# Gated experts: gathered rows split first, then turned by transposing DMA transfers instead of TensorE

## The reference, cut to what matters

```python
affinity = _sinkhorn(affinity_logits)
gates, idx = jax.lax.top_k(affinity, CAP)
expert_in = jnp.take_along_axis(x[:, None, :, :], idx[..., None], axis=2)
h = jax.nn.gelu(jnp.einsum('becd,edf->becf', expert_in, w1) + b1[None, :, None, :])
expert_out = jnp.einsum('becf,efd->becd', h, w2) + b2[None, :, None, :]
out = out.at[jnp.arange(b)[:, None, None], idx].add(gates[..., None] * expert_out)
```

## Time and profile before

| | us |
|---|---|
| median of 3 runs | 2324.47 |
| the profiled execution | 2321.31 |
| its span, first to last instruction | 2319.5 |
| TensorE busy in the span | 2096.1 (90%) |
| VectorE busy | 1494.0 (64%) |
| ScalarE busy | 1275.3 (55%) |
| GpSimd busy | 1095.1 (47%) |

### The profile page before, as it was taken

How to read it: one execution, slowest core, us unless ns; L and a number is a source line. 1 busy time by engine, 2 the same in 40 slices (tenths; PEclk the granted TensorE clock), 3 DMA queues, 4 the chain that set the end, 5 groups by cost and what they waited for, 6 DMA issues and landing times. The chain is left out here.

```text
span 2319.5 us, 47393 instructions
## 1 busy us (share of the span) xinstructions
PE 2096.1 (90%) x17558; PEld 1475.3 (64%) x17590; DVE 1494.0 (64%) x2938; ACT 1275.3 (55%) x2080; POOL 1095.1 (47%) x1263
## 2 busy tenths in 40 slices
PE   7799999996895599978999979965999999999998
PEld 5566666663664388855666658852676676676675
DVE  5677777775996755547888846666555555555553
ACT  2576666663443366535666645534645655655653
POOL 2888888841220222126666313403555355355343
PEclk9899999997998799999999989986999999999999
DMA  5000000000002233311111000042345345344332
GB/s 234 1 2 1 0 0 0 0 1 6 10 7 73 96 121 120 116 48 35 30 28 27 0 12 17 16 146 96 94 112 112 75 111 111 77 111 108 80 81 32
DMA packets 66925, 136.11 MB, mean 59 GB/s; under 512 B 11200, under 2 KB 52368, under 8 KB 59920
## 3 DMA queue, kind: packets, MB, share of 16 engines
q1 hardware_dynamic: 37264, 87.65, 11.2%
q0 software_dynamic: 29568, 47.21, 10.1%
HBM read 100.22 MB, written 34.60 MB: 58 GB/s over the span
## 5 line engine op out<-in xcount | busy, mean ns | idle before, releaser
L3448 ACT ACTIVATE f_h<-bank,f_b 128x512 f32<-128x512 f32 x256 | 176.0, 688 | 274.6 <-PE bank L176 268.0
L3545 DVE TENSOR_TENSOR f_hidlo<-f_h,f_hidhi 128x512 f16<-128x512 f32 x256 | 177.3, 692 | 174.0 <-ACT f_hidhi L3449 174.0
L176 PE MATMUL ring<-f_w2lo,f_hidhi 128*128 128x256 f16 x1024 | 279.1, 273 | 0.0
L176 PE MATMUL ring<-f_w2hi,f_hidhi 128*128 128x256 f16 x1024 | 279.1, 273 | 0.0
L176 PE MATMUL ring<-f_w2hi,f_hidlo 128*128 128x256 f16 x1024 | 279.1, 273 | 0.0
L3648 POOL DMA_INDIRECT out<-f_y,f_to_row x128 | 205.9, 1609 | 92.6 <-DVE f_y L3563 50.8
L176 PE MATMUL bank<-f_xthi,f_w1hi 128*128 128x512 f16 x512 | 194.7, 380 | 1.1 <-DVE f_xtlo L3524 1.1
L176 PE MATMUL bank<-f_xtlo,f_w1hi 128*128 128x512 f16 x512 | 194.8, 380 | 0.0
L176 PE MATMUL bank<-f_xthi,f_w1lo 128*128 128x512 f16 x512 | 194.7, 380 | 0.0
L3449 ACT ACTIVATE f_hidhi<-bank,f_b 128x512 f16<-128x512 f32 x256 | 174.2, 680 | 0.0
L3612 POOL DMA_INDIRECT f_xg<-tokens,f_from_row x128 | 143.8, 1123 | 48.4 <-issue 34.3
(11 more groups left out here) (639 smaller groups left out, 5971.6 us busy)
## 6 DMA issues: line engine op xcount, KB each, us to landing
f_raw<-in_e_w SPq DMA_DIRECT2D x32, 1024.0 KB, 5.7
c_raw<-in_e_w SPq DMA_DIRECT2D x16, 1024.0 KB, 7.1
slots_out<-c_y SPq DMA_DIRECT2D x40, 128.0 KB, 4.2
x<-in_x SPq DMA_DIRECT2D x1, 4096.0 KB
tokens<-c_xn SPq DMA_DIRECT2D x16, 256.0 KB, 2.6
tokens<-f_xn SPq DMA_DIRECT2D x16, 256.0 KB, 2.7
out<-x SPq DMA_DIRECT2D x1, 4096.0 KB, 15.1
wb<-in_wb SPq DMA_DIRECT2D x1, 3096.0 KB, 31.8
```

Of the source, the lines that this page charges most:

```text
L176: mm = pe.matmul(out, left[a], right[b], start=first and n == 0, stop=last and n == 2)
L3448: act.activation(h32[n % 4][:, :], src, ACT.Gelu_apprx_tanh, bias=bias).then_inc(sig["h_full"], 1)
L3545: dve.tensor_tensor(hid_v[1][:, it, at], h32[n % 4][:, :], hid_v[0][:, it, at], ALU.subtract).then_inc(sig["h_lo"], 1)
```

## The change

The rows of all experts but the first are split while they still lie as gathered, and the two float16 parts are turned by transposing DMAs that SyncE issues. `rows16`, two tiles of 128x2048 float16, lies in the tile `x`, which nothing reads any more. ScalarE writes the high part of `xg` there in two activations of 128x1024 (`high_rows`), VectorE the low part in two subtractions (`low_rows`); SyncE (`turn`) waits until the hidden products of the expert before have read `xt`, then for each part, and issues one transposing transfer of 128x2048 for each. TensorE waits for both (`xt_turned`) ahead of `hidden`. `turn_next` goes; GpSimd waits for the splits (`rows_low`) where it waited for the transposes. SyncE's loop over the experts is written out.

```diff
+        rows16 = [mem.x[:, k * KT * CT * P // 2:(k + 1) * KT * CT * P // 2].bitcast(F16) for k in range(2)]
...
-                each_expert(sp, E1, load)
+                def turn(e):
+                    sp.wait_ge(sig["h_made"], e.before * NH)
+                    for k, name in enumerate(("rows_high", "rows_low")):
+                        sp.wait_ge(sig[name], e.count(GROUPS, 0))
+                        sp.dma_start_transpose(xt[k][:, :].rearrange("p (c d) -> p c d", d=P), rows16[k]
+                                               ).then_inc(sig["xt_turned"], 16)
+
+                for n in range(E1 + 1):
+                    if n >= 2:
+                        turn(Turn(n - 1, n))
+                    if n < E1:
+                        load(n % 2, Turn(n, n + 1))
...
-                def turn_next(e):
-                    for c in range(GROUPS):
-                        turn_rows(Turn(e.now, e.now + 1), c, None)
-
                 def expert(p, e, more):
                     pe.wait_ge(sig["w1_free"], e.now)
+                    pe.wait_ge(sig["xt_turned"], e.count(32, 0))
                     for c in range(GROUPS):
-                        pe.wait_ge(sig["xt_ready"], e.count(4, 2 * c + 2))
                         hidden(e, c, range(IT))
-                    if more:
-                        turn_next(e)
                     outputs(p, e)
...
+                def high_rows(e, c):
+                    act.wait_ge(sig[f"gathered{c}"], e.count(16 * GT, 16 * GT))
+                    act.activation(rows16_v[0][:, :, GT * c:GT * c + GT, :], xg_v[:, :, GT * c:GT * c + GT, :], ACT.Copy
+                                   ).then_inc(sig["rows_high"], 1)
...
+                def low_rows(e, c):
+                    at = slice(GT * c, GT * c + GT)
+                    dve.wait_ge(sig["rows_high"], e.count(GROUPS, c + 1 - GROUPS))
+                    dve.tensor_tensor(rows16_v[1][:, :, at, :], xg_v[:, :, at, :], rows16_v[0][:, :, at, :], ALU.subtract
+                                      ).then_inc(sig["rows_low"], 1)
...
-                    pool.wait_ge(sig["turned"], e.count(4, 0))
+                    if split is None:
+                        pool.wait_ge(sig["turned"], 4)
+                    else:
+                        pool.wait_ge(sig["rows_low"], split * GROUPS)
```

More of the change, by code:

```diff
@@ L3317, in gated_experts @@
         w1_v, xt_v = ([tiles(t[:, :], KT) for t in parts] for parts in (w1, xt))
+        rows16_v = [t.rearrange("p (h c d) -> p h c d", h=KT, d=P) for t in rows16]
+        xg_v = xg[:, :].rearrange("p (c h d) -> p h c d", h=KT, d=P)
         hid_v = [tiles(t[:, :], IT) for t in hid]
@@ L3323, in _, with load @@
             def _(sp):
-                def load(p, e, more):
+                def load(p, e):
                     sp.wait_ge(sig["w1_free"], e.before)
@@ L3346, in turn_rows @@
                     for h in range(KT):
[L3347 to L3352, removed]
                         for j in range(GT):
                             ct = GT * c + j
-                            mm = pe.transpose(to[:, j * P:(j + 1) * P],
+                            mm = pe.transpose(banks[h][:, j * P:(j + 1) * P],
                                               xg[:, ct * D + h * P:ct * D + (h + 1) * P], mem.const("ident"))
@@ L3361, in hidden @@
                         n = IT * c + it
-                        if n >= 4:
+                        if n >= 4 or not isinstance(e.before, int) or e.before:
                             pe.wait_ge(sig["h_hi"], e.count(NH, n - 3))
@@ L3425, in take_gates, with high_first @@
                                        ).then_inc(sig["gates_read"], 1)
-                def high_rows(e, c, banks=None):
+                def high_first(c, banks):
                     for h in range(KT):
[L3429 to L3432, removed]
+                        act.wait_ge(sig["turned"], 2 * c + h + 1)
+                        act.activation(xt_v[0][:, h, c * HALF:(c + 1) * HALF], banks[h], ACT.Copy
+                                       ).then_inc(sig["xt_hi"], 1)
+                def high_rows(e, c):
+                    act.wait_ge(sig[f"gathered{c}"], e.count(16 * GT, 16 * GT))
+                    act.activation(rows16_v[0][:, :, GT * c:GT * c + GT, :], xg_v[:, :, GT * c:GT * c + GT, :], ACT.Copy
+                                   ).then_inc(sig["rows_high"], 1)
                 def high_w1(e):
@@ L3471, in first_expert @@
                     take_gates(0)
-                    high_rows(e, 0)
+                    high_first(0, bank[0:2])
                     gelus(0, e, 0, range(IT - 2))
-                    high_rows(e, 1, early_bank)
+                    high_first(1, early_bank)
                     gelus(0, e, 0, range(IT - 2, IT))
@@ L3516, in take_rows, with low_first @@
                         dve.tensor_copy(by_tile(rows, d, g), chosen(row_bank[g], d)).then_inc(sig["rows_read"], 1)
-                def low_rows(e, c, banks=None):
+                def low_first(c, banks):
                     for h in range(KT):
-                        tb = 2 * c + h
-                        src = bank[tb] if banks is None else banks[h]
                         at = slice(c * HALF, (c + 1) * HALF)
-                        dve.wait_ge(sig["xt_hi"], e.count(4, tb + 1))
-                        dve.tensor_tensor(xt_v[1][:, h, at], src, xt_v[0][:, h, at], ALU.subtract
+                        dve.wait_ge(sig["xt_hi"], 2 * c + h + 1)
+                        dve.tensor_tensor(xt_v[1][:, h, at], banks[h], xt_v[0][:, h, at], ALU.subtract
                                           ).then_inc(sig["xt_ready"], 1)
+                def low_rows(e, c):
[3 more added lines that the diff above has]
+                                      ).then_inc(sig["rows_low"], 1)
                 def low_w1(e):
@@ L3582, in first_expert @@
                     number_tokens(1)
-                    low_rows(e, 0)
+                    low_first(0, bank[0:2])
                     take_rows(1)
                     low_hidden(e, 0, range(IT - 2))
-                    low_rows(e, 1, early_bank)
+                    low_first(1, early_bank)
                     low_hidden(e, 0, range(IT - 2, IT))
@@ L3623, in gather_first, with gather @@
                     fetch(c)
-                def gather(e):
+                def gather(e, split):
                     for c in range(GROUPS):
                         pool.wait_ge(sig[f"gathered{c}"], e.count(16 * GT, 0))
-                    pool.wait_ge(sig["turned"], e.count(4, 0))
+                    if split is None:
+                        pool.wait_ge(sig["turned"], 4)
+                    else:
+                        pool.wait_ge(sig["rows_low"], split * GROUPS)
                     settle(pool, sig)
@@ L3653, in expert @@
                     if more == 2:
-                        gather(Turn(e.now + 1, e.now + 2))
+                        gather(Turn(e.now + 1, e.now + 2), e.now)
                     add(p, e)
@@ L3660, in _ @@
                 gather_first(1)
-                gather(Turn(1, 2))
+                gather(Turn(1, 2), None)
                 each_expert(pool, E1, expert)
```

## The result

The changed kernel takes 2294.24 us in the median, the kernel before 2323.76 in the runs beside it: a ratio of 0.9872 (0.9855 to 0.9888, a 95% interval as in all brackets that follow a ratio). One of the four executions of the changed kernel took 2514.65 us, at a mean granted clock of 0.82 against 0.96 in the three others, and is left out of the ratio. On the chip of the later runs it was 2292.39 against 2324.28, 0.9862 (0.9847 to 0.9877). The profiled execution took 2294.40 us where that of before took 2321.31, 26.9 less; the medians differ by 29.5. The profiled pair differs by less because the part ahead of the changed code took 3.3 us longer in the one than in the other: the first of the transposes that go stands at 1633.64 us before the change, and the outputs that take its place begin at 1636.98 with it.

The account below looks back on a forecast made before the run. TensorE was taken as the bound; 15 x 2.01 = 30.2 us of transposes leave its path, everything added staying hidden. From the median 2324.47 that gives 2294 us, 1.3% less; range 2288 to 2325 to hold 8 in 10.

Parts of the forecast that it names:

- The bound: In the experts, 1700 to 2200 us: TensorE busy 99.91 of 100 us, so its saved time is the kernel's.
- The gain: Between hidden products and outputs of 15 experts: TensorE's 16 transposes go, 2.01 us each time, 30.2 us in all.
- The transfers: SyncE's two 512 KB transposing transfers beside TensorE's outputs: 3.7 us each, landed by 10.9 us, ten microseconds early.
- The bound by pieces: Both transposing transfers as 4096 pieces, priced like the write of `x` to `out`: 15.1 us, in by 18.6, 2.4 early.
- the indirect queue's price: Far end for the transposing transfers: 127 ns a piece, 32.5 us for both, ending at 36.0, 15.0 us late.
- The bank wait: At the output banks VectorE's reads stay ahead of TensorE, 2.6 us left at the tightest place, so no wait.
- The transfers at the indirect queue's price: First rival, at the wait before `hidden`: transfers take 32.5 us, each expert waits 15.0 us, 2520 us; 12%.
- blocks turned one after another: Second rival, in the transfers: 32 blocks at 1.8 us take 57.6 us, end 40.1 late, 2896 us; 6%.
- The third: Rival: transfers land around 20, held up by gather packets or a late split; TensorE waits 1 to 2 us, 2309 to 2324; 5%.
- the fourth: Rival at the output banks: subtractions at three times 2.5 us make TensorE wait 2.4 us, 2327 to 2331; 2%.

Follow-up runs that it names:

- six in a row: Changed kernel with each of an expert's two transposing transfers issued three times, the copies into spare columns, TensorE waiting for all: 2402.17 us, ratio 1.0329.
- the run with the slower split: Changed kernel with each of VectorE's subtractions for the low rows made three times, twice into spare columns: 2314.07 us, ratio 0.9955.
- the run with four: Changed kernel with each of an expert's two transposing transfers issued four times, the copies into spare columns, TensorE waiting for all: 2519.29 us, ratio 1.0838.

## Why the prediction was right

*The bound.* TensorE was the bound of the experts and stays it; leaving out the transfers moved nothing, putting TensorE's old work back undid everything.

*The gain.* 15 x 2.01 = 30.2 us was the sum; the medians differ by 29.5, by 31.9 in the later runs, and the period fell by the 2.01 us read from the timeline. That the median came out at 2294 to the microsecond is luck.

*The transfers.* I took 7.4 us for the pair by a line through plain copies; its last packet ends 6.3 us after the first issue. No row of before had a transposing transfer, so that the price came so near was luck; nothing hung on it, with eleven microseconds to spare. The bound by pieces, 15.1 us, was far too high, and the indirect queue's price, 127 ns a piece, more so: 5.3 us of 16 engines over 4096 pieces are 21 ns each. What I did not price is the other traffic: six in a row come to 3.7 us each, of which the engines need 2.8 for the transfer and the rest goes to GpSimd's packets and to the two ends. My 3.7 us for 512 KB, six times from 3.5 on, would have given 25.7, the measured end, but for another reason.

*The bank wait.* A lead of 2.6 us was read from the rows of before; the run with the slower split gives 2.8. It is the nearer of the two limits, far nearer than the transfers'.

*The rivals.* The transfers at the indirect queue's price, and blocks turned one after another, are refuted by the 5.3 us for both. The third and the fourth needed a wait of TensorE, and it has none (100.00 of 100.00 us); the subtractions took 2.36 us where I had 2.5. The list in the Trainium skill, page "VectorE: DVE Perf Modes", section "The three transpose paths", gives 1309 ns for one 128x128 block by DMA; here 32 blocks took 5.3 us, 166 ns each in a row, so its figure cannot be multiplied. The 261 GB/s of its page "DMA: Bandwidth & Descriptors", section "Latency and other measured facts", is nearer: the pair had 198 GB/s, and a stretch of transposing packets alone in the run with four 0.28 MB in 1 us.

## What to carry to other kernels

Where one engine is busy without a break, read what each block of it costs from the start of one group to the start of the next, and look for an idle resource that can do the block inside a stretch where its result is not yet wanted. Then compute, for each engine that the move brings forward in time, how long the next buffer is still free: here the transfers had 11 us to spare, but VectorE only 2.8. Before planning with a transfer's price, ask what else the DMA engines do at that moment: in the row of six, 3.9 us of their 18.5 went to GpSimd's packets.

## What the runs showed of the hardware

A transposing transfer of 128x2048 float16 within SBUF keeps all 16 DMA engines busy for about 2.65 us (5.3 us for two), and SyncE's queue for 2.0 us when it is alone, and 2.50 behind another one. The issue of a plain 1 MB load took 0.33 us, and 0.83 right behind the transfers. Six transfers in a row kept the engines at the same price, 2.8 us each by their packets' time, while GpSimd's gather and adds took a fifth of the engines' time beside them. Within single microseconds one of the two queues was seen to have the engines nearly alone.
